# A gated cross-attention block with mixture-of-experts layers: VectorE's rounds of the second attention written out, the square root on ScalarE, and fetched and routed rows handled at other places

## The reference, cut to what matters

```python
x = x + tanh(g_xattn[0]) * L0_xattn(layernorm(x), ctx, ...)   # 32 heads of 8, rotary positions
x = x + tanh(g_ffn[0])   * L0_ffn(layernorm(x), ...)          # 8 experts, top 2, and a shared expert
x = x + tanh(g_xattn[1]) * L1_xattn(layernorm(x), ctx, ...)   # 16 heads of 128, 8 key/value heads
x = x + tanh(g_ffn[1])   * L1_ffn(layernorm(x), ...)          # 8 experts, top 2, tanh router
# layernorm(x) = (x - mean) / sqrt(var + 1e-5), over the 256 columns
```

## Time and profile before

| | |
|---|---|
| median of 3 runs | 1771.6 us (1771.45 to 1773.22) |
| the profiled execution's own time | 1754.08 us |
| its span, first to last instruction | 1752.2 us |
| TensorE (PE) busy | 1546.5 us, 88% |
| VectorE (DVE) busy | 1183.9 us, 68% |
| ScalarE (ACT) busy | 710.0 us, 41% |
| GpSimd (POOL) busy | 560.5 us, 32% |
| mean granted TensorE clock | 0.958 |

### The profile page before, as it was taken

How to read it: one execution, slowest core, us unless ns; L and a number is a source line. 1 busy time by engine, 2 the same in 40 slices (tenths; PEclk the granted TensorE clock), 3 DMA queues, 4 the chain that set the end, 5 groups by cost and what they waited for, 6 DMA issues and landing times.

```text
span 1752.2 us, 42290 instructions
## 1 busy us (share of the span) xinstructions
PE 1546.5 (88%) x14338; PEld 1310.1 (75%) x14338; DVE 1183.9 (68%) x3176; ACT 710.0 (41%) x1487; POOL 560.5 (32%) x682
## 2 busy tenths in 40 slices
PE   3899999978898899999779999989898989988987
PEld 2566666656776678899778888888788888877875
DVE  5888888886756665455467766666666666665876
ACT  2566666653222224555333333333332323344632
POOL 3555555531412230000111222222222222234556
PEclk8999999999999999999889999999999999989999
DMA  7566666661100013533300111001001001013635
GB/s 197 111 124 123 123 123 123 123 121 44 61 28 24 25 49 91 167 124 115 136 22 23 34 34 33 31 30 33 25 31 32 31 31 33 28 55 102 211 115 167
DMA packets 149017, 137.40 MB, mean 78 GB/s; under 512 B 12986, under 2 KB 138611, under 8 KB 148508
## 3 DMA queue, kind: packets, MB, share of 16 engines
q1 hardware_dynamic: 138076, 106.38, 24.6%
q0 software_dynamic: 10816, 29.54, 5.3%
HBM read 64.69 MB, written 71.19 MB: 78 GB/s over the span
## 4 chain that ended last, share of the span: by engine, by line
PE 55%; DVE 23%; issue 10%; ACT 5%; DMA 3%; SPq 2%; DVEq 1%; POOL 1%; ACTq 1%; POOLq 0%
PE bank L632 11%; PE bank L633 10%; PE bank L634 10%; PE bank L1143 4%; PE bank L694 3%; PE bank L703 2%; PE bank L1171 2%; PE bank L717 2%; PE bank L658 2%; PE bank L734 2%; DVE oT_b_lo L2548 1%; DVE probs_b L2690 1%; DVE rm_b L2687 1%; PE bank L721 1%; DVE x L2453 1%
## 5 line engine op out<-in xcount | busy, mean ns | idle before, releaser
L1848 POOL TENSOR_TENSOR probs_b<-probs_b,rs_b 128x512 f32<-128x512 f32 x64 | 66.8, 1044 | 448.1 <-DVE rs_b L2700 447.7
L1619 ACT ACTIVATE probs_b<-probs_b 128x512 f32<-128x512 f32 x64 | 40.4, 631 | 375.5 <-DVE probs_b L2690 375.5
L632 PE MATMUL bank<-xT_b_hi,m_hi 128*128 128x256 f32 x512 | 154.0, 301 | 19.2 <-ACT qT L1579 12.1
L632 PE MATMUL bank<-n_hi,oT_b_hi 128*128 128x256 f32 x512 | 155.2, 303 | 0.7 <-DVE x L2527 0.7
L633 PE MATMUL bank<-n_hi,oT_b_lo 128*128 128x256 f32 x512 | 150.8, 295 | 0.0
L634 PE MATMUL bank<-n_lo,oT_b_hi 128*128 128x256 f32 x512 | 150.3, 294 | 0.0
L633 PE MATMUL bank<-xT_b_hi,m_lo 128*128 128x256 f32 x512 | 145.8, 285 | 0.0
L634 PE MATMUL bank<-xT_b_lo,m_hi 128*128 128x256 f32 x512 | 145.7, 285 | 0.0
L1829 POOL DMA_INDIRECT xn_b<-sorted_y,place_of x62 | 60.3, 973 | 234.9 <-DMA sorted_y<-ys 182.3
L1143 PEld LDWEIGHTS bank<-ctxT_b,qT 128*128 128x128 f32 x1024 | 125.2, 193 | 2.7
L1389 ACT ACTIVATE probs_a<-probs_a 128x512 f32<-128x512 f32 x128 | 80.4, 628 | 113.8 <-DVE probs_a L2019 113.4
(11 more groups left out here) (397 smaller groups left out, 4682.1 us busy)
## 6 DMA issues: line engine op xcount, KB each, us to landing
sorted_x<-zeros SPq DMA_DIRECT2D x16, 2112.0 KB, 14.0
xg<-sorted_x SPq DMA_DIRECT2D x71, 128.0 KB, 2.1
sorted_y<-ys SPq DMA_DIRECT2D x71, 128.0 KB, 2.0
xg<-sorted_x SPq DMA_DIRECT2D x31, 256.0 KB, 3.0
sorted_y<-ys SPq DMA_DIRECT2D x31, 256.0 KB, 2.7
w_raw<-in_w SPq DMA_DIRECT2D x16, 408.0 KB, 3.8
x<-in_x SPq DMA_DIRECT2D x4, 1024.0 KB, 7.5
cx_raw<-in_ctx SPq DMA_DIRECT2D x32, 128.0 KB, 2.7
```

The costliest lines, as they stand in the source:

```text
L632: pe.matmul(dst, lh, rh, start=start, stop=False, skip_group_check=True)
L1848: pool.tensor_tensor(probs_b[b], probs_b[b], rs_b[:, b, :].unsqueeze(2).broadcast_to([P, G1, S]), ALU.mult).then_inc(s["b_probs"], 1)
```

## The change: what it does

1. VectorE's twelve routed rounds are written out; TensorE and ScalarE keep their loops of two rounds. Semaphore values and addresses on VectorE become constants.
2. At the end of rounds 0 to 13 the reciprocal root is no longer made by `rsqrt`. VectorE adds the epsilon (`deviation_b`), ScalarE takes the square root after `q_copy(7)` (`root_b`), and VectorE makes the reciprocal and the shift (`shift_of_b`) after `ptl(i, 3)`. The one-off use ahead of round 0 and in round 0 keeps `rsqrt`.
3. `add_tile(2i + 4)` moves ahead of `ptl(i, 0)`; `add_tile(2i + 5)`, the moments and the epsilon move ahead of `otl(i, 2)`. GpSimd issues both tiles' fetches after batch 1.
4. TensorE turns the routed rows one step later, after `project1(1, 0)`; `logits_f` follows `project1(1, 1)` and writes bank 7; `back_f` follows `queries1(i + 1, 0)`. ScalarE copies the context's high half before the routed rows' high half.
5. First MoE: the eight subtractions of the down weights on GpSimd are spread over scatters 5 and 6, one ahead of each pair of DMAs.

```diff
@@ TensorE, logits_f @@
-                    m = split3(bank[6][0:E, 0:2 * P], (f1["rw_hi"][:, k, 0:E], f1["rw_lo"][:, k, 0:E]),
+                    m = split3(bank[7][0:E, 0:2 * P], (f1["rw_hi"][:, k, 0:E], f1["rw_lo"][:, k, 0:E]),
@@ TensorE, attend1 @@
                 scores1(i, 1)
+                rest(project1, 1, 0)
                 if route is not None:
                     turn_f(i, route)
-                rest(project1, 1, 0)
                 scores1(i, 2)
                 ahead(turn_x1)
+                rest(project1, 1, 1)
                 if route is not None:
                     logits_f(i)
-                rest(project1, 1, 1)
+                ahead(queries1, 0)
                 if route is not None:
                     back_f(i)
-                ahead(queries1, 0)
                 scores1(i, 3)
@@ ScalarE @@
+            def root_b(i):
+                act.wait_ge(s["stats_ready"], i + 2)
+                act.activation(sd[:, 0:4], sd[:, 0:4], ACT.Sqrt).then_inc(s["scalar_steps"], 1)
...
                 expo(1)
-                if route is not None:
-                    xh_f(i)
...
                 act.activation(cx_hi, cx_raw, ACT.Copy).then_inc(s["b_cxh"], 1)
+                if route is not None:
+                    xh_f(i)
                 expo(2)
...
                 next_q(7)
+                if not late and not last:
+                    root_b(i)
@@ GpSimd, first MoE @@
+            def down_low(h, e):
+                pool.wait_ge(s["dn_hi"], h + 1)
+                pool.tensor_tensor(dn_lo[h][:, e:e + 2], dn_raw[h][:, e:e + 2], dn_hi[h][:, e:e + 2], ALU.subtract).then_inc(s["dn_lo"], 1)
...
                 for t in range(FT):
+                    if i in (5, 6):
+                        down_low(i - 5, 2 * t)
                     for c in range(TOP):
...
             for i in range(NF):
                 scatter(i)
-                if i in (4, 5):
-                    h = i - 4
-                    pool.wait_ge(s["dn_hi"], h + 1)
-                    for e in range(0, E, 2):
-                        pool.tensor_tensor(dn_lo[h][:, e:e + 2], dn_raw[h][:, e:e + 2], dn_hi[h][:, e:e + 2], ALU.subtract).then_inc(s["dn_lo"], 1)
@@ GpSimd, second attention @@
-                    if i + 2 < NA and b % 2 == 1:
-                        gather((i + 2) * 2 + b // 2)
+                    if i + 2 < NA and b == 1:
+                        gather((i + 2) * 2)
+                        gather((i + 2) * 2 + 1)
@@ VectorE @@
+            def deviation_b(i):
+                ve.tensor_scalar(sd[:, 0:4], mv_new[:, 0:4, 1], LN_EPS, None, ALU.add).then_inc(s["stats_ready"], 1)
+
+            def shift_of_b(i):
+                ve.wait_ge(s["scalar_steps"], H1 + i + 1)
+                st.done(ve.reciprocal(rr_b, sd[:, 0:4]))
+                st.wait()
+                st.done(ve.scalar_tensor_tensor(out=shift_b, in0=mv_new[:, 0:4, 0], scalar=-1.0, in1=rr_b, op0=ALU.mult, op1=ALU.mult))
+                st.wait()
...
                 ve.tensor_tensor(cx_lo, cx_raw, cx_hi, ALU.subtract).then_inc(s["b_cxl"], 1)
+                if more:
+                    add_tile(i * 2 + 4)
                 ptl(i, 0)
                 weigh(2)
                 weigh(3)
                 otl(i, 0)
-                if more:
-                    add_tile(i * 2 + 4)
                 ptl(i, 1)
...
                 if late:
                     table_f()
+                if more:
+                    add_tile(i * 2 + 5)
+                    moments_b(i + 2)
+                    deviation_b(i)
                 otl(i, 2)
                 ptl(i, 3)
                 if late:
                     places_f()
                 if more:
-                    add_tile(i * 2 + 5)
-                    stats_b(i + 2)
+                    shift_of_b(i)
...
-            with ve.Fori(1, NR // 2 + 1) as j:
-                st.loop(j, STEPS["b"], 1)
-                for u in range(2):
-                    attend1(j * 2 + u, route=u)
-            st.end(NR // 2 + 1)
+            for i in range(2, NR + 2):
+                attend1(i, route=i % 2)
```

More of the change, by code:

```diff
@@ L44 @@
          "f1": dict(norm=0, t0=1, t1=3, logits=4, back=5, largest=5, weigh=6, weights=8)}
-STEPS = {"a": 12, "b": 122}
+STEPS = {"a": 12}
 TOP = 2
@@ L1605, in tanh_f @@
                 act.wait_ge(s["g_back_psum"], NF + i - 2)
-                act.activation(g1["lT"][0:E, :], bank[6][0:E, 0:2 * P], ACT.Tanh).then_inc(s["g_logit_copied"], 1)
+                act.activation(g1["lT"][0:E, :], bank[7][0:E, 0:2 * P], ACT.Tanh).then_inc(s["g_logit_copied"], 1)
             def w1_high(n):
@@ L2469, in norm1, with moments_b @@
                 ve.sem_inc(s["b_xn_ready"], 1)
-            def stats_b(i):
+            def moments_b(i):
                 ve.wait_ge(s["c_added"], i * 2 + 2)
-                ve.sem_inc(s["passed"], 1)
                 for t in range(2):
-                    st.done(ve.bn_stats(bn[:, 4 + t, :], x[:, ds(i * 2 + t, 1), :].rearrange("p a d -> p (a d)")))
+                    st.done(ve.bn_stats(bn[:, 4 + t, :], x[:, i * 2 + t, :]))
                 st.wait()
-                ve.sem_inc(s["passed"], 1)
                 for t in range(2):
@@ L2481, in stats_b @@
                 st.wait()
+            def stats_b(i):
+                moments_b(i)
                 rsqrt(rr_b, shift_b, 0, 4)
+            def deviation_b(i):
[6 more added lines that the diff above has]
+                st.wait()
             ve.wait_ge(s["w0x_loaded"], 160)
```

## The result

The changed kernel takes 1716.6 us (median of 4 runs, 1715.3 to 1719.2), the kernel before on the same chip 1771.5: a ratio of 0.969, 95% interval 0.9675 to 0.9706. That is faster, 3.0 us above the forecast of 1713.6 and inside the range.

A forecast was written before the change was run, and what follows sets the result against it. TensorE bounds the kernel, through its waits in the second attention's routed rounds and the clock lost by waiting. Terms -50.8 + 6.5 - 8.4 - 5.3 = -58.0 us gave 1713.6 us (from the 1771.6 median), range 1698 to 1738.

The forecast's parts named there:

- Part 1: Second attention's routed rounds: turning routed rows after `project1(1, 0)` removes TensorE's waits at L1075 and their clock loss, -50.8 us.
- The condition on `centre(0)`: Routed rounds on VectorE: `centre(0)` must start when scores 0 are there, 2.3 us into the round; `resid1` ends at 6.6.
- All twelve waits go: Routed rounds, L1075: TensorE's 34.3 us of waits ahead of the routed rows' transposes vanish, with 16.5 us of clock loss.
- Part 2: VectorE's routed rounds written out: the 2.87 us of "issue" at the loop's turn go, counted inside the -50.8 us.
- Part 3: Root moved to ScalarE: 3.0 of 3.15 us ahead of `centre(0)` removed, 28 table loads fall in idle time, cost 0.
- Part 4: Around scores 3: later `back_f` lengthens the `q_copy(0)` wait, +6.5 us (bounds 0, 17); earlier `add_tile` ends the `ptl(i, 1)` wait, -8.4.
- Part 5: First MoE: spreading GpSimd's subtractions shortens TensorE's waits behind held VectorE work, -5.3 us, bounds 0 and -7.8.
- I charge one hold a block: First MoE: one subtraction holds VectorE for 1.25 us in each block, so 7.8 - 2 x 1.25 = 5.3 us are gained.
- The clock fell nowhere: Rival, routed rounds: the clock falls at TensorE's longer wait for `q_copy(0)` instead; price 16.5 us, 1730 us, chance 0.18.
- Root tables were not late: Rival, ScalarE: drain and loop turn make the first exponential 2.6 us late every second round; 15 us, 1729 us, chance 0.10.
- rounds do not alternate: Sign against the forecast, routed rounds: lengths that still alternate because of ScalarE's loop turn; no size of its own.
- straight code did not stall: Rival, VectorE's written-out rounds: instruction fetch stalls, two a round, cost 69 us; 1782 us, slower, chance 0.04.

## Why the prediction was right, and where it was not

- **Part 1, size.** Booked -50.8 us (34.3 wait, 16.5 clock). Late turn and written-out rounds together gave 50.8 in the routed rounds, rounds of 41.5 us. The size and the clock's share (18.3) hold, the exact match by luck, as shown above. The condition on `centre(0)` was stricter than needed: in that run it still starts 3.0 us after scores 0 begin, 1.0 later than in the changed kernel, and nothing waits for `resid1`.
- **Part 1, attribution.** The step that failed is "All twelve waits go", booked to the late turn. Alone it gives 20 us, the written-out rounds alone 34, and in the full change it gives nothing. My own numbers had it: with `centre(0)` at 2.3 us, `norm_f` is through by 8.3 and the early turn is due at 8.1. A wait of 0.2 us is left, and 0.2 was measured. I used the sum for the slack of the new place and did not ask what the old place would cost under the same conditions.
- **Part 2.** Inside the -50.8 as said, but it is the part that carries most: VectorE's loop turn delayed the round and lowered the clock. No stall on fetching straight code came, as the Trainium skill (Runtime: NRT & Kernel Launch, Instruction fetch mechanics) states and the trace bears out: no "issue" ahead of `centre` in the twelve rounds, against 15.4 us in 5 turns before. The 15.3 us of "issue" ahead of `rr_b` are something else: the reciprocal starts at 1043.02, 0.03 us after ScalarE's root ends (1042.78 + 0.21), so it waits for the root and the releaser wasn't inferred; 2.40 us of waiting for scores follow it, so it costs nothing.
- **Part 3.** Cost 0, and it was 0. The root took 0.21 us where I took 0.2. The Trainium skill (ScalarE: Activation LUTs, What ACT_TABLE_LOAD costs) would have 1.38 us of drain on each load; the trace does not agree here: ScalarE goes from root to load in 0.01 us. The part was not needed either, since the early rows free 0.97 us ahead of `centre(0)`.
- **Part 4.** The wait for `qT` grew from 0.79 to 1.17 us, I had 1.3; it costs 14.3 - 9.5 = 4.8 us, and the logits-early run took 4.2 back; booked +6.5. The router's steps before `centre(3)` are shorter with constants (1021.87 to 1024.2, 2.3 us, against 2.7 before), which I had named as the lower bound. The wait at L1171 went, all 8.4 us as booked, but not all by the early rows: 5.1 by the run that puts rows and fetches back; the other 3.3 had gone with the loop (5.1 us are left in the written-out rounds alone).
- **Part 5 failed.** "I charge one hold a block" gave -5.3; the first profile of the change shows three a block on TensorE's path, 4.9 us together, more than the 3.9 that were saved, and the clock fell on top: +2.9. Of the twelve blocks of all six profiles, seven have one hold of 1.6 us on the path, as charged, and give 0.9 to 2.5 us each where 2.7 were booked; five have all three and lose 0.6 to 1.7. The sum over two blocks is +2.9 to -3.5, the mean -1. The step took one hold as certain where the place of the subtractions left it to chance, and put the clock at nothing.
- **Sum.** Routed rounds -56.0, by their terms -34.3 of wait, -18.2 of clock, +4.8 and -8.4 (parts 1 and 4 booked -52.7), first MoE +2.9 in that profile (booked -5.3): -53 against -58. Carrying the 17.5 us between the profiled run and the median over unchanged was right; the same stretches appear in the second profile of before, and in the group in which before takes 1752 us, the run with the root on VectorE, with routed rounds as long as the changed kernel's, has the ratio 0.966, much like 0.969 where before takes 1772.
- **Rivals.** The clock fell nowhere: 1.00 in all rounds, with a wait of 1.17 us in each. I would not call that rival refuted, since with the rounds written out alone a wait of the same length, at another place, was followed by a fall in three rounds of twelve. Root tables were not late, rounds do not alternate, straight code did not stall.

What stays open: whether early rows alone, with neither late turn nor ScalarE's root, would give 493 us beside the written-out rounds. The 0.97 us of slack in the run with the root on VectorE says so, but it was not run. Open as well is why the clock fell behind some waits and not behind others of the same length.

## What to carry to other kernels

When several parts of a change cure the same wait, work out the deadline at the old place under the new conditions too; what is left of the wait there is all that the second cure can be worth. Test such parts both ways, alone in the old kernel and left out of the new one, since one way alone would have credited the late turn with 20 us or with 0. An operation that holds another engine should be tied to a place where that engine works off the path, by a wait on a certain step, and not left to fall behind transfers whose timing moves from one execution to the next.

## What the hardware showed that was not expected

- TensorE's waits of one length did not always have the same sequel. With the rounds written out alone, 1.18 to 1.26 us at L1075 in each of twelve rounds was followed by a full grant nine times, and by 0.50 to 0.55 over 3 us in three rounds in a row. In the earlier trace rows 1.56 us was followed by a grant of 0.55, while 1.67 in the round before was not. A grant of 0.55 lies mostly at the 1.2 GHz level. With waits shorter by a third of a microsecond, and no loop turn, the mean over the stage rose from 0.95 to 0.99.
- While one GpSimd subtraction of 1.28 us runs, even a VectorE instruction on 128 x 4 numbers is held, 1.81 to 2.03 us instead of 0.17 (in one case from 582.35 to 584.38, beside the subtraction's 583.03 to 584.34). Four in a row held one VectorE subtraction for 5.61 and 5.91 us, their whole length: it got no turn between them. Spread, several can each take their own toll, but the one beside VectorE's `bn_stats` takes none (1.41 us for four, as without it).
- ScalarE switched table, took a root and switched back in 2.79 us, with nothing between them.
- In nine of the fourteen profiles, of either kernel, ScalarE stands 15 to 20 us at one place of the first MoE, its release shown as "remote", and resumes about when GpSimd's run of sixteen indirect transfers ends (452.84 and 453.01 us in the changed kernel's first profile). That is a coincidence in time only; nothing was run on it.
